# Cross-attention of a decoder layer: V stationary, exponentials moving, denominators from a stationary of ones, clips on GpSimd, batches written out

## The reference, cut to what matters

```
hat_x = layernorm(x);   lat = hat_x * ln_l_w + ln_l_b
hat_c = layernorm(ctx); cx  = hat_c * ln_c_w + ln_c_b
q = lat @ Wq            # 256 x 1024
k, v = cx @ Wk, cx @ Wv # 256 x 1024 each
for each head h:        # 64 columns of q, k, v
    E = clip(exp(q_h @ k_h.T / 8), exp(-11), exp(11))
    o_h = (E @ v_h) / rowsum(E)
x = layernorm(x + concat(o) @ Wo + bo)
```

## Time and profile before

| | |
|---|---|
| median of 3 runs | 2756.03 us (2754.13 to 2757.0) |
| the profiled execution | 2754.92 us, its span 2753.0 us |
| PE busy | 2539.5 us, 92% of the span |
| DVE busy | 1936.2 us, 70% |
| ACT busy | 1727.3 us, 63% |
| POOL busy | 1421.8 us, 52% |
| cross-attention stage | from about 342 us to about 705 us after the span's start |

### The profile page before, as it was taken

The page is one execution under the profiler, slowest core; times in us unless marked ns, Lnnn a source line. Parts: engine busy times, 40 slices in busy tenths (PEclk is TensorE's granted clock), DMA queues, the critical chain, the costliest instruction groups (busy, mean ns, idle before and its releaser), DMA issues.

```text
span 2753.0 us, 63692 instructions
## 1 busy us (share of the span) xinstructions
PE 2539.5 (92%) x23125; PEld 1733.6 (63%) x23125; DVE 1936.2 (70%) x3151; ACT 1727.3 (63%) x3268; POOL 1421.8 (52%) x1238
## 2 busy tenths in 40 slices
PE   6888699999799999999999999999999999999995
PEld 3444367777466666666666666666666666666664
DVE  5999844445577777777777777777777777777773
ACT  6778433333467666666666666667666666667663
POOL 3556400000466656656656656656656656656651
PEclk8999999999899999999999999999999999999997
DMA  2312110000112212212212212212212212212211
GB/s 73 101 57 59 43 41 0 0 0 0 31 46 65 57 48 66 57 48 67 57 47 67 57 47 67 57 47 67 57 47 67 58 47 67 58 47 67 58 47 44
DMA packets 102886, 140.06 MB, mean 51 GB/s; under 512 B 63040, under 2 KB 63936, under 8 KB 102336
## 3 DMA queue, kind: packets, MB, share of 16 engines
q1 hardware_dynamic: 102848, 139.57, 19.1%
HBM read 56.39 MB, written 1.31 MB: 21 GB/s over the span
## 4 chain that ended last, share of the span: by engine, by line
issue 30%; POOL 26%; PE 10%; DVE 5%; ACT 1%; POOLq 1%; DMA 0%; DVEq 0%; SPq 0%; ACTq 0%
POOL f_qkr L1266 8%; POOL f_qkr L1273 5%; POOL f_Pr L1248 5%; POOL f_qkr L1265 5%; DVE f_m L1462 4%; PE f_psA L1631 4%; PE f_psD L1725 3%; POOL f_tab L1256 2%; PE f_psO L1615 2%; PE f_psP L1594 2%; ACT f_sq L1340 1%; POOL xall L1287 1%; POOLq L1256 0%; POOLq L1287 0%; PE f_psD L1635 0%
## 5 line engine op out<-in xcount | busy, mean ns | idle before, releaser
L1248 POOL TENSOR_TENSOR f_Pr<-f_Pr,f_rden 128x384 f32<-128x384 f32 x384 | 310.8, 830 | 701.9 <-DVE f_rden L1441 701.9
L1462 DVE TENSOR_TENSOR f_m<-f_psA,f_tab 128x1024 f32<-128x1024 f32 x384 | 452.6, 1219 | 244.3 <-ACT f_sq L1340 244.2
L1631 PE MATMUL f_psA<-f_W,f_xT 128*128 (+1 forms) x1152 | 606.4, 619 | 16.9 <-issue 10.0
L1273 POOL TENSOR_TENSOR f_qkr<-f_qkr,f_rn 128x1024 f32<-128x1024 f32 x192 | 361.0, 1901 | 0.3 <-DVE f_rn L1491 0.3
L1340 ACT ACTIVATE f_sq<-f_psA 128x512 f32<-128x512 f32 x384 | 229.0, 596 | 145.6 <-PE f_psA L1631 139.2
L1594 PEld LDWEIGHTS f_psP<-ident,f_Pr 128*96 128x96 f32 x1536 | 165.9, 127 | 219.8 <-POOL f_Pr L1248 150.8
L1315 ACT ACTIVATE f_PT<-f_psP 96x512 f32<-96x512 f32 x384 | 227.0, 591 | 87.3 <-PE f_psP L1594 76.2
L1265 POOL TENSOR_TENSOR f_qkr<-f_m 128x512 f32<-128x512 f32 x192 | 244.9, 1275 | 55.9 <-DVE f_m L1462 55.7
L1631 PEld LDWEIGHTS f_psA<-f_W,f_xT 128*128 128x128 f32 x1152 | 183.3, 195 | 141.5 <-issue 63.6
L1615 PE MATMUL f_psO<-f_PT,f_V 96*64 96x64 f32 x6144 | 264.5, 229 | 3.4
L1430 DVE TENSOR_REDUCE f_mx<-f_psS 128x8 f32<-128x768 f32 x192 | 179.6, 935 | 122.8 <-PE f_psS L1578 122.8
(11 more groups left out here) (158 smaller groups left out, 4460.7 us busy)
## 6 DMA issues: line engine op xcount, KB each, us to landing
f_V<-f_Vt SPq DMA_DIRECT2D x96, 384.0 KB, 4.2
f_V<-f_Vt SPq DMA_DIRECT2D x96, 256.0 KB, 3.5
f_W<-in_f_W SPq DMA_DIRECT2D x48, 344.0 KB, 3.0
m_Cb<-m_BC_rows SPq DMA_DIRECT2D x64, 256.0 KB, 3.1
f_W<-in_f_W SPq DMA_DIRECT2D x48, 296.5 KB, 3.6
f_V<-f_Vt SPq DMA_DIRECT2D x48, 128.0 KB, 4.5
f_xsA<-xall SPq DMA_DIRECT2D x97, 32.0 KB
f_xsA<-xall SPq DMA_DIRECT2D x97, 31.8 KB
```

Source lines behind the costliest of these rows:

```text
L1248: pool.tensor_tensor(pv, pv, rv.unsqueeze(3).broadcast_to([P, 2, 2, KEYS]), ALU.mult).then_inc(Pr_ready[g][j], 1)
L1273: pool.tensor_tensor(qv, qv, rn[:, j * H:(j + 1) * H].unsqueeze(2).broadcast_to([P, H, DH]), ALU.mult).then_inc(qkr_ready[j], 1)
L1462: dve.tensor_tensor(m12[:, j, :, half].rearrange("p m (h d) -> p m h d", d=DH), psA[n % 2][:, :].rearrange("p (h d) -> p h d", d=DH).unsqu ...
L1631: pe.matmul(psA[n % 2][:, :], xT[:, t, :], weights(i, W_QKV + n * 512, 512), start=True, stop=True).then_inc(A_full[n_fill], 1)
```

## The change

The three streams are rewritten and a fourth is added on POOL.

1. **times_v.** V is now stationary (128 keys x 64 features) and `E` moving (256 queries). The two heads of a chunk write to partitions 0 to 63 and 64 to 127 of one bank, so the result has features on the partitions. There are four such matmuls per chunk. The denominators come from two more, with a 128x64 stationary of ones and, moving, `Es`, the sum of the two key tiles of `E`. They arrive in all 64 partitions of their head.
2. **POOL** does the clips (L764 of the changed kernel), the sum `Es` (L771) and the bias (L777).
3. **DVE** takes the reciprocal of 128x256 denominators and multiplies once, into `OT` directly. The transposes of `On`, their copies on ACT and the column of ones in V are gone.
4. **No loop:** all 64 chunks are written out. `latT`, `ctxT`, V and `OT` have two buffers, and batch b's remainder is spread over batch b+1: the output projection in chunks 1 and 2, its residual on DVE in chunk 2, the last rows in chunk 4. The next batch's row transposes come in chunk 3, its V in chunks 4 to 7.
5. The bank of a `psM` fill follows from the position in a list of all fills (`place`).

The core of the diff (lines of the kernel before that are listed above are not shown again):

```diff
-        V1 = sb("x_V1", [P, TPB, H, DH + 1])
+        V1 = sb("x_V1", [P, 2, TPB, H, DH])
-        E = sb("x_E", [P, 4, TPB, L])
-        On = sb("x_On", [P, TPB, H, DH])
+        E = sb("x_E", [P, 2, 2, TPB, L])
+        Es = sb("x_Es", [P, 2, 2, L])
+        rden = sb("x_rden", [P, 2, L])
+        OT = sb("x_OT", [P, 2, NC, L])
...
+        fills = [(0, "cat"), (0, "qk0")]
+        for g in range(CHUNKS + 1):
+            b, c = divmod(g, NC)
+            if g + 1 < CHUNKS:
+                fills.append(((g + 1) // NC, f"qk{(g + 1) % NC}"))
+            if g == 0:
+                fills += [(0, f"v{n}") for n in range(4)]
+            if c == 1 and b >= 1:
+                fills.append((b - 1, "wo"))
+            if c == 3 and b + 1 < B:
+                fills.append((b + 1, "cat"))
+            if c >= 4 and b + 1 < B:
+                fills.append((b + 1, f"v{c - 4}"))
+        fills.append((B - 1, "wo"))
+        place = {f: (k % 2, k // 2) for k, f in enumerate(fills)}
...
+            def clip(g, j):                       # POOL
+                pool.wait_ge(E_exp, 2 * g + j + 1)
+                pool.tensor_scalar(E[:, g % 2, j, :, :], E[:, g % 2, j, :, :], LO, HI, ALU.max, ALU.min).then_inc(E_ready, 1)
+            def sum_of_tiles(g):
+                pool.wait_ge(E_ready, 2 * g + 2)
+                if g >= 2:
+                    pool.wait_ge(O_full, g - 1)
+                pool.tensor_tensor(Es[:, g % 2, :, :], E[:, g % 2, :, 0, :], E[:, g % 2, :, 1, :], ALU.add).then_inc(Es_ready, 1)
...
+            def exponentials(g):                  # ACT
+                for j in range(2):
+                    act.wait_ge(S_full, 2 * g + j + 1)
+                    if j == 0 and g >= 2:
+                        act.wait_ge(O_full, g - 1)
+                    act.activation(E[:, g % 2, j, :, :], psS[(2 * g + j) % 4][:, :, :], ACT.Exp, scale=DH ** -0.5).then_inc(E_exp, 1)
...
+            def normalise(g):                     # DVE
+                dve.wait_ge(O_full, g + 1)
+                chain(dve.reciprocal(rden[:, g % 2, :], psO[g % 2][:, 1, :]))
+                dve.tensor_tensor(OT[:, g // NC % 2, g % NC, :], psO[g % 2][:, 0, :], rden[:, g % 2, :], ALU.mult).then_inc(O_free, 1)
...
+            for g in range(CHUNKS + 1):
+                b, c = divmod(g, NC)
+                if g + 1 < CHUNKS:
+                    copy_qk(g + 1)
+                if g >= 1:
+                    normalise(g - 1)
+                if c == 0 and b + 1 < B:
+                    statistics(b + 1)
+                if c == 2 and b + 1 < B:
+                    hats(b + 1)
+                if c == 2 and b >= 1:
+                    residual(b - 1)
+                if c == 4 and b >= 1:
+                    finish(b - 1)
...
+            def times_v(g):                       # PE
+                b, c = divmod(g, NC)
+                pe.wait_ge(E_ready, 2 * g + 2)
...
+                if g >= 2:
+                    pe.wait_ge(O_free, g - 1)
+                for kt in range(TPB):
+                    for j in range(2):
+                        pe.matmul(psO[g % 2][j * DH:(j + 1) * DH, 0, :], V1[:, b % 2, kt, 2 * c + j, :], E[:, g % 2, j, kt, :],
+                                  start=(kt == 0), stop=(kt == TPB - 1), skip_group_check=True)
+                pe.wait_ge(Es_ready, g + 1)
+                for j in range(2):
+                    ins = pe.matmul(psO[g % 2][j * DH:(j + 1) * DH, 1, :], ones[:, :], Es[:, g % 2, j, :], start=True, stop=True, skip_group_check=True)
+                ins.then_inc(O_full, 1)
...
+            for g in range(CHUNKS + 1):
+                b, c = divmod(g, NC)
+                if g + 1 < CHUNKS:
+                    project(g + 1)
+                if g < CHUNKS:
+                    scores(g)
...
+                if g >= 1:
+                    times_v(g - 1)
+                if c == 1 and b >= 1:
+                    out_projection(b - 1, 0)
+                if c == 2 and b >= 1:
+                    out_projection(b - 1, 1)
+                if c == 3 and b + 1 < B:
+                    transpose_rows(b + 1)
+                if c >= 4 and b + 1 < B:
+                    project_v(b + 1, c - 4)
```

More of the change, by code:

```diff
@@ L684, in cross_attention_block @@
         loaded = inputs.loaded
+        ones = sb("x_ones", [P, DH])
         stats = sb("x_stats", [P, R, 6])
@@ L759, in _ @@
-            rsqrt_of_variance(0)
-            scale_transposed(0)
[L761 to L781, removed]
@@ L783, in _ @@
+            deviation2(B - 1)
         @block.vector
         def _(dve):
-            dve.sem_inc(misc_free[0], 1)
-            dve.sem_inc(misc_free[1], 1)
-            dve.memset(V1[:, :, :, DH:DH + 1], 1.0).then_inc(ones_ready, 1)
+            dve.memset(ones[:, :], 1.0).then_inc(ones_ready, 1)
             dve.wait_ge(loaded, LOADS)
[L790 to L799, removed]
-                ins.then_inc(hat_ready, 1)
@@ new lines, in residual, with finish @@
+            def residual(b):
+                ps, free = wait_fill(dve, b, "wo")
+                dve.wait_ge(res_ready, b + 1)
+                dve.tensor_tensor(res[:, :, :], res[:, :, :], ps[:, 0:TPB * D].rearrange("p (t d) -> p t d", d=D), ALU.add).then_inc(free, 1)
+                wait_evacuated(dve, b, "wo")
+                layer_norm_stats(dve, passed, mom2_ready, chain, [res[:, j, :] for j in range(TPB)], stats2, mom2)
+            def finish(b):
+                dve.wait_ge(rstd2_ready, b + 1)
+                for j in range(TPB):
+                    ins = dve.tensor_scalar(xall[:, b * TPB + j, :], res[:, j, :], mom2[:, j, 0:1], rstd2[:, j:j + 1], ALU.subtract, ALU.mult)
+                ins.then_inc(finished, 1)
@@ L850, in _ @@
+            residual(B - 1)
+            finish(B - 1)
         @block.tensor
@@ new lines, in scores @@
+            def scores(g):
+                wait_evacuated(pe, g // NC, f"qk{g % NC}")
+                for j in range(2):
+                    h = 2 * g + j
+                    if h >= 4:
+                        pe.wait_ge(E_exp, h - 3)
+                    r = slice(j * DH, (j + 1) * DH)
+                    for kt in range(TPB):
+                        ins = pe.matmul(psS[h % 4][:, kt, :], qk[r, g % 2, 1, kt * P:(kt + 1) * P], qk[r, g % 2, 0, :], start=True, stop=True)
+                    ins.then_inc(S_full, 1)
@@ new lines, in out_projection @@
+            def out_projection(b, t):
+                if t == 0:
+                    pe.wait_ge(O_free, (b + 1) * NC)
+                    ps, full = bank(b, "wo")
+                else:
+                    j = place[b, "wo"][0]
+                    ps, full = psM[j], misc_full[j]
+                for c in range(NC):
+                    ins = pe.matmul(ps[:, t * D:(t + 1) * D], OT[:, b % 2, c, t * P:(t + 1) * P], wo[:, c, :], start=(c == 0), stop=(c == NC - 1))
+                if t == TPB - 1:
+                    ins.then_inc(full, 1)
```

249 lines of the change are left out of this document (113 added, 136 removed).

## The result

| | before | changed |
|---|---|---|
| device time, median of 4 runs | 2756.52 us (2754.13 to 2757.94) | 2779.48 us (2777.04 to 2780.28) |
| ratio, 95% interval | | 1.0083 (1.0065 to 1.0101) |
| profiled execution, span | 2754.9, 2753.0 | 2778.7, 2776.8 |

A forecast was written before the change was run, and what follows sets the result against it. PE was taken to set the pace: batches of 35.6 us PE work plus seven 2.3 us waits end the stage at 657.8, 47.3 us earlier, giving 2709 us; own range 2701 to 2717, with rivals 2693 to 2729.

The forecast's parts named there:

- POOL's clip: One clip of 512 elements on POOL: forecast 1.04 us, bounds 0.43 and 2.55.
- rival A: POOL decides: each clip costs two passes, 2.55 us, a POOL batch 53.5 us, end near 2830; chance 0.05.
- the prediction's own formula: POOL's time per batch is 8 x (2C + 1.5) + 0.7 us, with C the time of one clip.
- slower than before: POOL's batch passes the 44.2 us of before from a clip of 1.97 us on.
- Rival C: In chunk 2 POOL slows DVE's four row operations by 1.5 us; PE waits 3.8, time 2720; chance 0.15.
- the wait: At chunk 3, PE waits 2.3 us for DVE's residual to free the output projection's bank, seven times, 16.1 us.
- rival D: DVE's reciprocal is priced as an ordinary operation: waits of 1.0 us a batch, time 2699; chance 0.12.
- normalise: DVE's reciprocal, multiplication and two semaphore hops: 2.25 us, in chunk 2 ending 0.65 after PE stopped.
- Rival B: Column halves don't overlap in times_v: 2.7 us, a chunk 1.3 more, +83 in all, time 2792; chance 0.04.
- rival F: Waits of 2 to 5 us a batch, POOL's late sums among them, time 2728 to 2750; chance 0.06.
- rivals E: Nothing gained: the spreading opens new unseen waits of 6 us a batch, time 2755; chance 0.03.

The follow-up runs named there:

- the long clip: Changed kernel with both heads' clips in one POOL operation of 128x1024 in place of two of 512: 2784.82 us, one run.
- the kernel without the wait: Changed kernel, clips on DVE, output projection's second half before chunk 2's scores, residual before DVE's clips and row operations: 2692.24 us, ratio 0.9774.

## Why the prediction was wrong

**The step that failed is POOL's clip: "I take 1.04."** It is 1.915. The bounds (0.43 and 2.55) held it; the value between them didn't. I drew it from L1273, whose second operand is repeated, and read its lower price as the price of one stream. One-input POOL operations lie above the two-input ones: 1.485 with one ALU operation and 1.915 with two, against 1.27. "Streams and not arithmetic set POOL's price" was the argument against rival A; the clip with one operation refutes it, and the measured 1.915 the two passes of rival A (2.55). Nor is the clip long because DVE gets in its way: 128 clips take 1.914 to 1.917 us each in the kernel before with its clips moved, and 1.913 to 1.983 in the changed one. With 1.915 the prediction's own formula gives 8 x (3.83 + 1.5) + 0.7 = 43.3 us a batch in place of 37.9: 43 of the 72 us between this kernel and the one with clips on DVE.

The Trainium skill has for this clip the line that the prediction names (GPSIMD Engine Reference, section 4.1: two-input operations about twice VectorE's time, one-input ones roughly line-rate). The clip disagrees with it: 1.915 against DVE's 0.425, 4.5 times. The estimate of 0.6 us from it was further off than my own.

**The second step that failed is that a bound engine has no gaps.** I put "slower than before" at 1.97 us a clip, from POOL's sum alone. At 1.915 it is slower already. Two measured points, 2733.07 at 1.485 (one run, one ALU operation) and 2779.48 at 1.915, put the crossing with 2756 near 1.70 on a straight line, which is an estimate. What the formula lacks is 45.4 to 47.1 less 43.3, that is 2 to 4 us a batch (1.2 in one) in which POOL waits for exponentials because PE did boundary work first. Over the six steps between the first matmuls of batches two to eight (the first is 45.6) this is 16.8 us of the other 29, and some 5 of them are the lower clock of three batches. The rest lies at the stage's two ends: from the last batch's L924 to the next stage it is 82.7 us, against 63.6 with the clips on DVE, as PE has no next batch to prepare there and POOL is as slow as ever.

**Rival A** (POOL decides, 0.05) had the right place and the wrong size. Its chance was too small for a term whose two bounds, 0.43 and 2.55, lay on either side of the crossing, and whose value came from an argument and not from a row of that form of operation.

**Rival C** (DVE held by POOL, 0.15) is real where POOL has work at that moment. My ground against it, that PE's wait starves POOL just then, is refuted by the kernel with one clip on each engine (a pair of row operations at 1.17, PE's wait 0.57 longer) and by the long clip. In the changed kernel it costs little: the rows above show a pair of row operations at 0.59. Its price was misread too. The 718 ns of L457 is a mean of unlike operations: the 16 have a median of 336 ns and a longest of 2391. Four of them, with POOL idle, took 1.11 us together:

```profile
340.93 1.11 DVE L457 TENSOR_SCALAR xall<-m_res,m_mom,m_rstd 128x128 f32<-128x128 f32 x4 [0.60 <-ACT m_rstd L288]
```

Each other group of four has one that lasts about as long as the POOL operation beside it (L250, 2.38 us). So a row operation costs its 0.34 us, or what is left of POOL's instruction, and not 0.72. The Trainium skill's SBUF — State Buffer, in "SBUF: two separate sides" on the shared port pair, has an exclusive hold for the whole instruction; these rows agree, and so do the row operations that end with POOL's clip and with its sum, 507.98 and 509.34.

**What came out.** With the clips on DVE: times_v 1.44 (1.40 forecast), column halves side by side; the batch 37.97 (37.9); the stage's end 658.3 (657.8); 2707.3 us (2709). Part of that closeness is luck. PE's work in a batch is 36.06 us, as the kernel without the wait shows, where I had 35.6; and the wait costs 37.97 - 36.06 = 1.91 where I had 2.3. The two misses cancel. The last output projection takes 5.67 us in the changed kernel (4.64 forecast). The reciprocal is 1.758 us (1.74), so the slope from the earlier trace rows was the right reading and rival D is out. The profile has PE's wait for the residual at 1.69 (1.78 to 1.81 in the changed kernel), which doesn't count the last matmuls' latency. It is shorter than forecast mainly because normalise is done 0.37 us after PE's part of that half, and not 0.65, an estimate from the starts of the rows (473.51 + 1.88 for PE, 475.76 for the first row operation); the row operations take 1.02 (1.12). Rival B is out by times_v. Two slips in the sums change nothing: a slope of 8 ns gives a reciprocal of 2.2 us and not 2.3, and rival F's 2 to 5 us a batch give some 2725 to 2749. No wait of rivals E and F was seen with the clips on DVE.

## What to carry to other kernels

Before work moves to GpSimd, price the very form of operation there, with its inputs and its ALU operations; a value picked inside a range whose ends lie on either side of the break-even decides nothing. Here the clips' 72 us outweighed the 47 that the rest gained. An engine that joins a chain of hand-overs needs slack against the serial work of the others: here a POOL load of 36.5 us beside PE's 37.9 already stretched the batch to 40.4 at the full clock, and to 41.6 in the mean. And after such a change look for the one engine that took over the pace, put back only that part, and keep the rest.

## What was not expected of the hardware

- On POOL, `tensor_scalar` on 128x512 f32 takes 1.485 us with one ALU operation and 1.915 with two, 3.624 on 128x1024: 3.34 ns an element. `tensor_tensor` on 128x512, with two inputs, takes 1.27.
- DVE's reciprocal of 128x256 takes 1.758 us against 0.424 for a multiplication of that size.
- PE matmuls on the two column halves overlap whatever their order (batches of 37.97 and 38.01, the second from one run).
- A row operation of DVE on SBUF (128x128) takes 0.34 us or waits for POOL's instruction to end: pairs of 0.59, 1.17, 1.54 and 2.15 us were seen.
- The granted clock has a price beside the waits, and doesn't follow their length alone. A batch at 0.96 is some 1.6 us longer than one at 1.00, with the clips on POOL (47.0 and 45.4), with one clip on each engine (40.3 and 38.7) and without clips (39.6 and 38.0). The same half output projection took 3.56 us, at 0.50 in its first 2 us, or 2.05, behind the same two waits of PE. What decides between the two wasn't tried.
